# Layer 0's attention: scores computed a second time with keys on partitions, the exponential read from PSUM, and no transposes of the probabilities

## The chip, the core and the metric

The kernel runs on one NeuronCore of a Trainium2 chip. Its time is the device time of one execution in microseconds (us); the time of a kernel is the median of its runs. TensorE is called PE below, VectorE DVE, ScalarE ACT, GpSimd POOL and SyncE SP.

## The reference, cut to what matters

Two layers, each with an attention over a context and a mixture of eight experts, work on 128 sequences of 64 tokens of 128 features. The change is in the first attention, which has 16 heads of 8 features:

```python
qh = _split_heads(q @ w_q + b_q, N_HEAD)      # q = _layernorm(x)
kh = _split_heads(k @ w_k + b_k, N_HEAD)      # k = v = ctx_1024
vh = _split_heads(v @ w_v + b_v, N_HEAD)
scores = jnp.einsum('bhqd,bhkd->bhqk', qh, kh) / jnp.sqrt(jnp.float32(d_k))
attn = jax.nn.softmax(scores, axis=-1)
context = jnp.einsum('bhqk,bhkd->bhqd', attn, vh)
...
x = x + jnp.tanh(g_xattn[0]) * (context @ w_out + b_out)
```

After it come the experts of layer 0 (each token is routed to its best two), the attention of layer 1 and its experts. All is float32.

## The kernel before, in words

The 8192 tokens are 64 tiles of 128 tokens (two sequences each). The attention of layer 0 goes over `NP` = 32 pairs of tiles, in a loop `for p in range(NP + 3)` that stands once in the program of each engine, in an order written out by hand; each engine runs its own list from top to bottom, and semaphores join them. Every second turn prepares a group of four tiles: `turn` transposes the normalised tokens, `project_q` and `project_k` multiply, ACT adds the bias, and POOL's `keys` writes four masked copies of the keys into `kx`.

For a pair of tiles the work before the change is this. `scores(p)` (L474) puts queries on partitions: 16 matmuls of 32 rows and 64 columns of weights into PSUM banks 0 to 3, which hold 128 x 2048 scores. DVE takes the largest of each row of 64 keys (`largest`, L954) and subtracts it (`shift`, L961) while it copies the scores to SBUF, so that the four banks are free again for `scores(p + 1)`. ACT takes the exponential in place (`exponentials`, L1449). POOL adds the two halves of each row (`fold`, L1723), DVE sums what is left and inverts it (`denominators`, L967 and L970). PE transposes the probabilities, 16 times 128 x 128 (`turn_p`, L486), ACT copies them out of PSUM in four pieces (`copy_p`, L1456), and one turn later PE multiplies them with the values (`attend`, L501: 32 matmuls with 32 columns of weights and 64 moving columns). The reciprocals are spread by ACT (`spread_rden`, L1461), transposed (`turn_rden`, L509), copied (`copy_rden`, L1467), multiplied in (`normalise`, L976), and `output` (L516 for the bias, L520) and `add_output` (L981) end the pair. `values` is L459, `turn` L433, `turn_router0` L535 (tokens transposed for the router), `logits` L568, `project_q` L441, `project_k` L448.

Beside it DVE runs `stats0` and `stats_router` (L945, L950), and in turns 13 to 18 and 25 to 30 the steps of `route0`, which chooses the experts of the tokens that are ready; `ROUTE` says how many steps a turn gets, and where in it. From turn 19 on DVE's `put_rows` (L939) and POOL's `put` (L1734, two indirect DMAs for a tile) send out the first 16 tiles. POOL also turns sums into mean and deviation (`moments`, L1692 to L1701). Turns are named below by the `p` of `scores(p)`.

## Time and profile before

| | us |
|---|---|
| median of 3 runs | 1210.59 (1209.36 to 1211.75) |
| the profiled execution, its own time | 1206.6 |
| its span | 1204.8 |
| PE, DVE, ACT, POOL busy | 1047.8, 658.3, 641.6, 537.8 |
| first to last start of `largest` (L954) | 21.6 to 331.6 |

The span is what the instructions cover; the own time is 1.8 us more. Busy times are sums over the whole span and say little of one stage. The rows further down are read by stage: the attention of layer 0 fills the span from about 20 to 350 us.

### The profile page before, as it was taken

The page shows a single profiled execution, that of the slowest core. Times are in us where ns is not written, and L with a number is a line of the kernel's source. Part 1 is how long each engine was busy: PE and PEld are TensorE (multiplying, and loading weights), DVE is VectorE, ACT ScalarE, POOL GpSimd, SP SyncE. Part 2 cuts the span into 40 slices and gives each one's busy share as a digit, 9 for nine tenths or more (in the row PEclk, how much of TensorE's full clock was granted, in tenths as well). Part 3 has the DMA queues.
Part 4 walks back from the last instruction along what each step waited for, and adds up shares of the span by engine and source line. Part 5 has one row for each costly group of instructions (what it writes and reads, how often), then busy time and mean ns, then how long its engine had stood idle before and what let it go on. Part 6 is the DMA issues. An engine that isn't in the chain of part 4 may idle for free.

```text
span 1204.8 us, 26712 instructions
## 1 busy us (share of the span) xinstructions
PE 1047.8 (87%) x9578; PEld 882.3 (73%) x9578; DVE 658.3 (55%) x1673; ACT 641.6 (53%) x1488; POOL 537.8 (45%) x767
## 2 busy tenths in 40 slices
PE   4888877887689899999999756779999999999988
PEld 1676755665579899998998645657777877877866
DVE  3888899779955722224554746774435434533311
ACT  2888876776555454454465633435445445444433
POOL 5555664887357777723771767330220131111100
PEclk9999998998889999999999977889999999999999
DMA  9800000000045576666665211000000000000000
GB/s 375 350 2 2 3 2 2 24 22 21 10 155 176 190 231 204 188 199 194 186 202 196 110 27 35 5 1 1 1 10 15 13 10 10 10 19 9 10 18 27
DMA packets 74819, 98.30 MB, mean 82 GB/s; under 512 B 10051, under 2 KB 49219, under 8 KB 73283
## 3 DMA queue, kind: packets, MB, share of 16 engines
q1 hardware_dynamic: 65202, 75.42, 18.3%
q0 software_dynamic: 8192, 16.79, 4.7%
q10 hardware_dynamic: 1296, 4.39, 0.9%
q8 instruction: 79, 1.29, 0.4%
q14 instruction: 50, 0.40, 0.1%
HBM read 36.45 MB, written 32.11 MB: 57 GB/s over the span
## 4 chain that ended last, share of the span: by engine, by line
PE 59%; DVE 12%; ACT 9%; POOL 9%; issue 7%; DMA 2%; SPq 1%; POOLq 0%; DVEq 0%; ACTq 0%
PE psum L821 10%; PE psum L811 10%; PE psum L654 9%; PE psum L644 9%; PE psum L843 4%; POOL work L1749 3%; PE psum L792 2%; PE psum L831 2%; ACT w_sb L1449 2%; PE psum L800 2%; POOL rstd L1700 1%; DVE mx L954 1%; ACT work L1456 1%; PE psum L568 1%; PE psum L634 1%
## 5 line engine op out<-in xcount | busy, mean ns | idle before, releaser
L1539 ACT ACTIVATE hid_sb<-psum,work 128x128 f32<-128x128 f32 (+1 forms) x424 | 145.7, 411 | 146.0 <-PE psum L644 141.4
L1749 POOL DMA_INDIRECT work<-yg,place x128 | 129.4, 1011 | 105.8 <-DMA yg<-yg_sb 62.2
L1800 POOL TENSOR_TENSOR ctx_sb<-ctx_sb,chosen_sb 128x272 f32<-128x272 f32 x64 | 43.5, 681 | 292.4 <-DVE ctx_sb L1339 281.4
L644 PE MATMUL psum<-work 128*128 128x128 f32 (+1 forms) x848 | 152.0, 323 | 4.7 <-issue 2.8
L654 PE MATMUL psum<-w_sb,hid_sb 128*128 x1192 | 151.3, 276 | 0.4 <-DVE yg_sb L1146 0.4
L1641 ACT ACTIVATE work<-psum,w_sb 128x272 f32<-128x272 f32 x256 | 115.1, 487 | 65.2 <-PE psum L811 64.9
L654 PEld LDWEIGHTS psum<-w_sb,hid_sb 128*128 128x128 f32 x1192 | 145.7, 193 | 2.7 <-issue 0.6
L644 PEld LDWEIGHTS psum<-work 128*128 128x128 f32 x848 | 125.2, 194 | 14.9 <-issue 4.5
L811 PE MATMUL psum<-work,w_sb 128*128 128x272 f32 x512 | 130.1, 396 | 4.2 <-ACT work L1641 3.8
L1146 DVE TENSOR_TENSOR yg_sb<-psum,b_sb 128x128 f32<-128x128 f32 (+1 forms) x106 | 36.6, 346 | 171.7 <-PE psum L654 170.5
L821 PE MATMUL psum<-work,w_sb 128*128 128x272 f32 x512 | 127.8, 392 | 0.0
L1357 DVE TENSOR_SCALAR work<-psum,b2T_sb 128x272 f32<-128x272 f32 x64 | 32.1, 501 | 157.3 <-PE psum L821 157.3
L1723 POOL TENSOR_TENSOR fold_sb<-w_sb 128x1024 f32<-128x1024 f32 x32 | 75.5, 2361 | 83.1 <-ACT w_sb L1449 74.8
L821 PEld LDWEIGHTS psum<-work,w_sb 128*128 128x128 f32 x512 | 97.2, 190 | 20.0
L1734 POOL DMA_INDIRECT xg<-work,place x96 | 93.7, 976 | 29.7 <-issue 21.0
L811 PEld LDWEIGHTS psum<-work,w_sb 128*128 128x128 f32 x512 | 87.6, 190 | 25.7 <-ACT work L1641 5.6
L1456 ACT COPY work<-psum 128x512 f32<-128x512 f32 x128 | 69.2, 588 | 46.0 <-PE psum L486 45.1
L954 DVE TENSOR_REDUCE mx<-psum 128x32 f32<-128x2048 f32 x32 | 73.0, 2282 | 5.9 <-PE psum L474 5.7
L961 DVE TENSOR_TENSOR w_sb<-psum,mx 128x2048 f32<-128x2048 f32 x32 | 73.0, 2281 | 0.2
L1649 ACT COPY ctx_sb<-psum 102x256 f32<-102x256 f32 x64 | 23.8, 373 | 91.8 <-PE psum L831 91.6
L486 PE MATMUL psum<-ident,w_sb 128*128 128x128 f32 x512 | 71.4, 286 | 0.3 <-ACT w_sb L1449 0.3
L1422 ACT COPY lnT<-psum 128x512 f32<-128x512 f32 x64 | 37.9, 593 | 51.7 <-PE psum L433 27.9
(219 smaller groups left out, 2006.4 us busy)
## 6 DMA issues: line engine op xcount, KB each, us to landing
work<-w_sb SPq DMA_DIRECT2D x106, 258.0 KB
work<-xg SPq DMA_DIRECT2D x73, 128.0 KB
yg<-yg_sb SPq DMA_DIRECT2D x73, 128.0 KB
xg<-yg_sb SPq DMA_DIRECT2D x24, 384.0 KB, 10.5
out_x<-x_sb SPq DMA_DIRECT2D x16, 256.0 KB, 2.0
x_sb<-in_x SPq DMA_DIRECT2D x3, 1024.0 KB, 16.1
ctx_sb<-in_ctxT ACTq DMA_DIRECT2D x3, 1024.0 KB, 17.1
w_sb<-in_w1a SPq DMA_DIRECT2D x1, 2064.0 KB, 15.1
```

Of the source, the lines that this page charges most:

```text
L644: e.matmul(banks[UP_BANKS[c]][:, 0:cols], w1g_sb[:, b % NW, c * P:c * P + P], xgT_sb[:, u % 2, at:at + cols], start=True, stop=True).then_ ...
L654: ins = e.matmul(banks[DOWN_BANKS[b % 2]][:, n * D:n * D + D], hid0[:, b % 2, c, n * P:n * P + P], w2_sb[:, bass.ds(number, 1), c, :].rear ...
L811: e.matmul(banks[b][:, 0:TS * SLOTS], w1_sb[:, ex, c * P:c * P + P], xgT[sg % 2][:, ex, :, :].rearrange("p t s -> p (t s)"), start=True, s ...
L821: ins = e.matmul(banks[3][:, 0:TS * SLOTS], w2_sb[:, ex, c, :], hid[:, ex % 2, c, :, :].rearrange("p t s -> p (t s)"), start=(c == 0), sto ...
L954: e.tensor_reduce(mx[:, p % 2, :], four_banks, AX_X, ALU.max).then_inc(s_mx, 1)
L961: e.tensor_tensor(pr[:, i, :, :, :, :].rearrange("p j u h k -> p (j u h) k"), four_banks, mx[:, i, :].unsqueeze(2).to_broadcast([P, 2 * HE ...
L1456: e.copy(pT[:, p % 2, u, 4 * half:4 * half + 4, :], banks[B_T[half]]).then_inc(s_pT, 1)
L1539: e.activation(hid0[:, b % 2, c, 0:cols], banks[UP_BANKS[c]][:, 0:cols], ACT.Gelu, bias=w1g_sb[:, b % NW, HID + c:HID + c + 1]).then_inc(s ...
L1641: e.activation(hid[:, ex % 2, c, :, :].rearrange("p t s -> p (t s)"), banks[(HC * ex + c) % 3][:, 0:TS * SLOTS], ACT.Gelu, bias=w1_sb[:, e ...
L1723: e.tensor_tensor(folded, flat[:, :, 0:S // 2], flat[:, :, S // 2:S], ALU.add).then_inc(s_fold, 1)
L1734: e.indirect_dma_start(xg_dram[h], at, src, None, bounds_check=NROWS[h] - 1, oob_is_err=False).then_inc(s_put[i], 16)
L1749: e.indirect_dma_start(dst[:, k, :], None, yg_dram[h], at, bounds_check=NROWS[h] - 1, oob_is_err=False).then_inc(s_get[i], 16)
```

## The change

The scores are still computed once with queries on partitions, for their maxima only. `largest` now writes the negative maxima; PE transposes them (`turn_maxima`, one 128 x 128), DVE copies them (`copy_maxima`), and `turned_scores` computes the scores again with keys on partitions: for each of four column ranges of the four banks a matmul of a constant 0/1 table `own_max` (32 rows, 128 columns of weights, 128 moving columns, in four row groups) puts the negative maximum of each query there, and two matmuls in each row group (32 rows, 128 columns of weights from `kx`, 64 moving columns from `qT`) add the scores on top. ACT takes the exponential straight from PSUM, all four banks in one instruction, and writes the probabilities as `attend` wants them. `shift`, `turn_p`, `copy_p` and `fold` are gone. The sums over keys are now made by PE (`denominators`, 32 matmuls with the table `own_head`), DVE inverts 128 x 64 of them (`invert`), POOL spreads them over a table (`part_rden`), and a matmul with `own_dims` (`spread_rden`) takes the place of `turn_rden`. `scores(p)` now waits for the exponential of the turn before, since that is what frees banks 0 to 3. The output bias is added to the rows of x by POOL (`bias_rows`), and its matmul is gone. `add_output` comes one turn later, `attend` one turn sooner. The tables are three loads more on ACT's queue; w2 is loaded at the start instead of at the end of the attention.

```diff
             def scores(p):
                 g, i = p // 2, (p // 2) % 2
                 w.wait_ge(s_qe, g + 1)
                 w.wait_ge(s_kx, g + 1)
-                w.wait_ge(s_sub, p)
+                w.wait_ge(s_exp, p)
...
-            def turn_p(p, chunks):
-                i = p % 2
-                w.wait_ge(s_exp, p + 1)
-                for n in chunks:
-                    u, half = n // 2, n % 2
-                    w.wait_ge(s_pT, 4 * p + n - 1)
-                    for r in range(4):
-                        pair = 4 * half + r
-                        ins = e.transpose(banks[B_T[half]][:, r * P:r * P + P], pr[:, i, pair // 2, u, 2 * (r % 2):2 * (r % 2) + 2, :],
-                                          ident[:])
-                    ins.then_inc(s_pt, 1)
+            def turn_maxima(p):
+                w.wait_ge(s_mx, p + 1)
+                w.wait_ge(ld["ident"], 64)
+                e.transpose(banks[B_M][:, 0:P], mx[:], ident[:]).then_inc(s_mt, 1)
+
+
+            def turned_scores(p):
+                i = (p // 2) % 2
+                w.wait_ge(s_mT, p + 1)
+                for u in range(2):
+                    t = 2 * (p % 2) + u
+                    for h in range(2):
+                        at = 256 * u + 128 * h
+                        for quad in range(QUADS):
+                            q = slice(32 * quad, 32 * quad + 32)
+                            e.matmul(banks[quad][:, at:at + P], own_max[q, u, h, :], mxT[q, :], start=True, stop=False)
+                        for b in range(2):
+                            c = t * P + b * S
+                            for quad in range(QUADS):
+                                q = slice(32 * quad, 32 * quad + 32)
+                                ins = e.matmul(banks[quad][:, at + b * S:at + b * S + S],
+                                               kx[q, i, 2 * t + b, 2 * h:2 * h + 2, :].rearrange("p j k -> p (j k)"),
+                                               qT[q, i, c:c + S], start=False, stop=(b == 1))
+                ins.then_inc(s_sub, 1)
...
-            def turn_rden(p):
+            def denominators(p):
                 i = p % 2
-                bank = banks[B_C]
+                w.wait_ge(s_rden, p)
+                for r in range(PAIRS):
+                    for u in range(2):
+                        for b in range(2):
+                            row = 32 * (2 * u + b)
+                            ins = e.matmul(banks[B_M][row:row + 32, P:P + S], own_head[:, r, :], pT[:, i, r // 2, u, r % 2, b * S:b * S + S],
+                                           start=(r == 0), stop=(r == PAIRS - 1))
+                ins.then_inc(s_dd, 1)
+
+            def spread_rden(p):
                 w.wait_ge(s_rdm, p + 1)
-                for u in range(2):
-                    ins = e.transpose(bank[:, 256 + u * P:256 + u * P + P], rdm[:, i, u * P:u * P + P], ident[:])
-                ins.then_inc(s_av, 1)
+                e.matmul(banks[B_C[p % 2]][:, 256:512], own_dims[:, 0:P], rdm[:, p % 2, :], start=True, stop=True).then_inc(s_rt, 1)
...
             def exponentials(p):
-                flat = pr[:, p % 2, :, :, :, :].rearrange("p j u h k -> p (j u h k)")
+                flat = pT[:, p % 2, :, :, :, :].rearrange("p j u h q -> p j (u h q)")
                 w.wait_ge(s_sub, p + 1)
-                e.activation(flat, flat, ACT.Exp, scale=SCALE0).then_inc(s_exp, 1)
+                w.wait_ge(s_dd, p - 1)
+                e.activation(flat, psum[:, 0:4, :], ACT.Exp, scale=SCALE0).then_inc(s_exp, 1)
```

The order of an engine's list, as the compiled programs have it. First PE, turn 8 of the loop before, from `scores` (L474) to the transposes of the next group (L433); each row is the line, the operation, what it writes and reads, and partitions by columns of the output:

```order
L474 MATMUL psum<-work 64x256 x16
L568 MATMUL psum<-wrc,lnT 128x8 x4
L501 MATMUL psum<-work,hid_sb 32x64 x32
L459 MATMUL psum<-w_sb,ctx_sb 64x2x32 x8
L509 MATMUL psum<-ident,rdm 128x128 x2
L486 MATMUL psum<-ident,w_sb 128x128 x8
L448 MATMUL psum<-ctx_sb,w_sb 128x512
L516 MATMUL psum<-bias_sb,ones_row 128x256
L520 MATMUL psum<-w_sb,ctxn 128x128 x2
L486 MATMUL psum<-ident,w_sb 128x128 x8
L433 MATMUL psum<-ident,ln_sb 128x128 x4
```

And PE of the changed kernel, the first part of an odd turn (`scores` is L471 there, `logits` L583, `attend` L511, `turn` L430, `denominators` L523, `values` L456, `turn_maxima` L478, `turned_scores` L490 and L495):

```order
L471 MATMUL psum<-work 64x256 x16
L583 MATMUL psum<-wrc,lnT 128x8 x4
L511 MATMUL psum<-work,hid_sb 32x64 x32
L430 MATMUL psum<-ident,ln_sb 128x128 x4
L523 MATMUL psum<-work,own_head 32x64 x32
L456 MATMUL psum<-w_sb,ctx_sb 64x2x32 x8
L478 MATMUL psum<-ident,mx 128x128
L490 MATMUL psum<-mxT,own_max 128x128 x4
L495 MATMUL psum<-work 128x64 x8
```

The last two rows stand there four times in turn. Between `scores` and the maxima's transpose there is now all of `logits`, `attend`, `turn`, `denominators` and `values`; an even turn has `turn_router0` in place of `turn` and no `logits`. Behind the last of the turned scores the list goes on to the next turn (project, `spread_rden` L529, `output` L534):

```order
L495 MATMUL psum<-work 128x64 x8
L445 MATMUL psum<-ctx_sb,w_sb 128x512
L529 MATMUL psum<-rdm,own_dims 128x256
L534 MATMUL psum<-w_sb,ctxn 128x128 x2
L471 MATMUL psum<-work 64x256 x16
```

Only these three stand between the turned scores and the next `scores`, which waits for the exponential. DVE, one turn before the change:

```order
L954 TENSOR_REDUCE mx<-psum 128x32
L976 TENSOR_TENSOR ctxn<-psum,ctxn 128x256
L961 TENSOR_TENSOR w_sb<-psum,mx 128x2048
L981 SCALAR_TENSOR_TENSOR x_sb<-psum,tg_sb,x_sb 128x256
L967 TENSOR_REDUCE den<-fold_sb 128x32
L970 RECIPROCAL rden<-den 128x4x2x4
L945 BN_STATS stats<-x_sb 128x6 x2
L950 BN_STATS stats<-x_sb 128x6 x2
```

and the same turn of DVE in the changed kernel:

```order
L996 SCALAR_TENSOR_TENSOR x_sb<-psum,tg_sb,x_sb 128x256
L975 TENSOR_REDUCE mx<-psum 128x4x8
L980 COPY mxT<-psum 128x128
L985 RECIPROCAL rden<-psum 128x64
L990 TENSOR_TENSOR ctxn<-psum,ctxn 128x256
L963 BN_STATS stats<-x_sb 128x6 x2
L968 BN_STATS stats<-x_sb 128x6 x2
```

Two long passes (L961 and L967) are gone from it, a short copy and a longer reciprocal are new, and the steps of `route0` all stand behind the last row.

## Rows read from the trace of the kernel before

**Rows 1.** Windows by stage: busy us (instructions) of each engine, then granted clock, DMA.

```profile
21.62:81.60 59.98, 48.58 (x848) 36.26 (x852) 48.94 (x62) 45.75 (x85) 33.58 (x48) 0.91 0.60 235
81.60:134.64 53.04, 46.86 (x892) 37.07 (x884) 44.99 (x62) 43.37 (x82) 36.03 (x59) 1.00 0.01 2
134.64:331.65 197.01, 152.34 (x2632) 118.72 (x2624) 174.76 (x290) 130.60 (x241) 120.99 (x153) 0.92 0.04 13
331.65:354.15 22.50, 17.65 (x308) 15.15 (x298) 15.30 (x37) 12.24 (x24) 9.88 (x20) 0.95 0.52 178
```

**Rows 2.** One line's instructions: ns min/median/max, first and last start us.

```profile
L954 DVE TENSOR_REDUCE mx<-psum x32: 2261/2280/2293, 21.6 to 331.6; 128x32 f32<-128x2048 f32 x32
```

**Rows 3.** Groups by line, 50 to 330 us: busy us, mean ns, idle before.

```profile
L1723 POOL TENSOR_TENSOR fold_sb<-w_sb 128x1024 f32<-128x1024 f32 x28 | 66.1, 2360 | 62.1 <-ACT w_sb L1449 54.9 <-DVE den L967 5.1 <-issue 1.7
L961 DVE TENSOR_TENSOR w_sb<-psum,mx 128x2048 f32<-128x2048 f32 x28 | 63.9, 2281 | 0.1
L486 PE MATMUL psum<-ident,w_sb 128*128 128x128 f32 x448 | 62.2, 285 | 0.0
L1456 ACT COPY work<-psum 128x512 f32<-128x512 f32 x112 | 60.5, 588 | 43.1 <-PE psum L486 42.3
L1449 ACT ACTIVATE w_sb<-w_sb 128x2048 f32<-128x2048 f32 x27 | 51.6, 1912 | 0.0
L1715 POOL TENSOR_SCALAR work<-work,vec_sb 128x512 f32<-128x512 f32 x52 | 35.3, 694 | 16.5 <-ACT work L1434 16.3
L1734 POOL DMA_INDIRECT xg<-ln,place x32 | 32.4, 1012 | 10.2 <-issue 7.2 <-POOL nmr L1701 2.5 <-DVE ln L939 0.3
L1700 POOL TENSOR_TENSOR rstd<-ln_tmp,minus_half 128x8 f32<-128x8 f32 x12 | 20.0, 1667 | 1.0
L976 DVE TENSOR_TENSOR ctxn<-psum,ctxn 128x256 f32<-128x256 f32 x28 | 11.8, 423 | 17.6 <-ACT ctxn L1467 17.4
L970 DVE RECIPROCAL rden<-den 128x32 f32<-128x32 f32 x27 | 9.5, 353 | 0.9
```

**Rows 4.** Timeline, PE: start us, length us, instructions (records) merged, idle before.

```profile
103.09 1.12 PE L441 MATMUL psum<-lnT,w_sb 128*128 128x512 f32 x2 [0.23 <-ACT hid_sb L1443]
104.48 0.61 PE L520 MATMUL psum<-w_sb,ctxn 128*128 128x128 f32 x4
104.93 1.04 PE L486 MATMUL psum<-ident,w_sb 128*128 128x128 f32 x8
105.80 0.60 PE L535 MATMUL psum<-ident,x_sb 128*128 128x128 f32 x4
106.33 1.12 PE L474 MATMUL psum<-work 32*64 32x256 f32 x32
107.38 0.97 PEld L568 LDWEIGHTS psum<-wrc,lnT 128*128 128x128 f32 x8 [0.39 <-ACT lnT L1422]
108.37 1.10 PE L501 MATMUL psum<-work,hid_sb 128*32 128x64 f32 x64
110.12 0.69 PE L459 MATMUL psum<-w_sb,ctx_sb 128*64 128x64 f32 x16 [0.66 <-ACT lg_sb L1476]
110.74 0.44 PE L509 MATMUL psum<-ident,rdm 128*128 128x128 f32 x2
...
115.52 1.12 PE L474 MATMUL psum<-work 32*64 32x256 f32 x32
116.57 1.10 PE L501 MATMUL psum<-work,hid_sb 128*32 128x64 f32 x64
117.60 0.55 PEld L459 LDWEIGHTS psum<-w_sb,ctx_sb 128*64 128x64 f32 x16
```

**Rows 5.** Timeline, the first turns.

```profile
29.21 2.01 PE L474 MATMUL psum<-work 32*64 32x256 f32 x32
...
31.33 2.29 DVE L954 TENSOR_REDUCE mx<-psum 128x32 f32<-128x2048 f32 x1 [4.74 <-PE psum L474]
```

More of the change, by code:

```diff
@@ L588, in tensor_program @@
             for p in range(NP + 3):
[L589 removed]
                 if p < NP:
                     scores(p)
+                if p % 2 == 1 and 0 <= (p - 7) // 2:
+                    w.wait_ge(s_wrc, 1)
+                    logits((p - 7) // 2, ROUTER, B_P, wrc[:, 0:NE], s_lnTr, s_lgm, s_lg)
+                for h in range(NPARTS - 1):
+                    if p == routing_start(h) + 4:
+                        count0(h)
+                if 0 <= p - 1 < NP:
+                    attend(p - 1)
```

310 lines of the change are left out of this document (148 added, 162 removed).

## The prediction

> **What bounds the kernel now.** I read the windows by stage first. The attention of layer 0 runs from the first `largest` at 21.6 us to the last at 331.6 us: 310.0 us for 31 turns, 10.0 us each [rows 2]. It has two halves. In turns 6 to 12, where no routing runs, 53.04 us for six turns is 8.84 us a turn, and PE, DVE and ACT are all busy for 43 to 47 of the 53 us: no single engine is the bound, they hand over to each other [rows 1]. From 134.64 to 331.65 us there are 18 turns of 10.94 us, and DVE is busy for 174.76 of 197.01 us: the steps of `route0` and `put_rows` lie on top of a DVE that was already nearly full, and PE's granted clock falls to 0.92 because it waits [rows 1]. Then 22.5 us pass until the experts begin [rows 1]; everything later is untouched but for the order of a few small instructions.
>
> **What leaves the engines.** Per turn DVE loses `shift` (2.28 us) and the sum over 1024 columns (half the width, so about 1.2), ACT loses four copies of 0.588, POOL the fold of 2.36, and PE 16 transposes [rows 3]. New on DVE are a 128 x 128 copy (below the 0.42 of the 128 x 256 row L976; I take 0.3) and a reciprocal of 64 columns instead of 32 (between 0.35 and 0.71; I take 0.55) [rows 3]. DVE's quiet turn of 44.99 / 6 = 7.50 us busy becomes 7.50 - 2.28 - 1.2 - 0.35 + 0.3 + 0.55 = 4.5, ACT's 43.37 / 6 = 7.23 becomes 7.23 - 2.35 = 4.9 [rows 1]. Neither is a bound any more.
>
> **What comes onto PE.** For the pace I use the starts of neighbours in the timeline [rows 4]. `scores` takes 1.05 us of PE's list (115.52 to 116.57), `attend` 1.03 (116.57 to 117.60), `logits` 0.99 (107.38 to 108.37), four transposes 0.53 when another tile shape follows (105.80 to 106.33), `values` 0.62 (110.12 to 110.74). `denominators` has the form of `attend` (32 columns of weights, 64 moving columns, 32 of them): 1.03. A matmul of 512 moving columns is 0.86 (its record of 1.12 less the tail of about 0.25 that others show), so `spread_rden` with 256 is 0.43, and `output` 0.45 (104.48 to 104.93).
>
> `turned_scores` has no like in the trace. A float32 matmul leaves two records, and small shapes run side by side in as many places as the array can be cut into: L474 has 32 records of 256 moving columns in eight places, so four rounds, and lasts 1.12; L501 has 64 records of 64 columns in four places, 16 rounds, and lasts 1.10. That is 0.216 us for a round of 256 columns and 0.056 for one of 64, plus a tail near 0.2 [rows 4]. The turned scores are 48 matmuls, 96 records in four places: 8 rounds of 128 moving columns (0.11 each) and 16 of 64. If the moving columns set the pace, they last 8 x 0.11 + 16 x 0.056 + 0.2 = **1.95 us**. But each of them loads 128 columns of weights, where L474 loads 64 and L501 only 32. The nearest row for many weights and few moving columns is L568: 8 loads of 128 columns in front of only 8 moving columns take 0.97 us, 0.11 a record, although eight moving columns are nearly nothing [rows 4]. With that pace all 24 rounds cost 0.11: 2.66 + 0.2 = **2.85 us**. I take this one, since L568 is the only row in which the loads are the longer part. The upper end is that the loads of the four row groups don't run side by side either: 96 x 0.11 = 10.5 us. L474 speaks against it: 32 loads in a row of half that width (0.055) would be 1.8 us, and the whole of it lasted 1.12.
>
> The skill has a rule that would make this worse. The Trainium skill ("TensorE: Matmul & The Clock Gate", Part 3, What overlaps and what doesn't) says that a weight load overlaps a running matmul only where the row group differs; each row group here reloads for its own next matmul. By that rule a round costs load plus matmul, 0.11 + 0.11 or 0.11 + 0.056. The trace does not agree: in L520 the four records of 128 columns, all in the same rows, follow each other in 0.45 us, 0.11 each, with loads as wide as the matmuls [rows 4].
>
> **The new loop.** Before, banks 0 to 3 were free after `shift`; now one turn holds them until the exponential has read them. So one turn is a closed chain, and nothing of the next turn's scores can start sooner: `scores`, what stands behind them on PE, the maxima's transpose, the copy, the turned scores, the exponential. `largest` itself ends 1.1 + 2.3 = 3.4 us after the start of `scores`, sooner than PE gets to the transpose:
> - even turn: 1.05 + 1.03 + 0.53 + 1.03 + 0.62 = 4.26 us (3.73 in turns 2 and 4, which turn nothing for the router); odd turn from 7 on, with `logits`: 5.25.
> - then transpose 0.28, copy 0.3, turned scores 2.85, exponential 1.91 [rows 3, 4] and four or five handovers, 0.14 in all: 5.48.
> - the project, the spread and the output (0.86 + 0.43 + 0.45 = 1.74) lie under the exponential; without that cover they would cost those 1.74.
>
> Sum: **9.74 us** for an even turn, **10.73** for an odd one from 7, 9.21 in turns 2 and 4, against 8.84 in the quiet stretch and 10.94 in the routed one.
>
> Turn 0 is longer. Its turned scores run while PE has the 1.2 GHz level, at which L474 took 2.01 instead of 1.12 [rows 5]: about 5.3 us. Behind them stand, one after another, the group's transpose copy, `project_k`, its bias, `project_q` and `scores(1)`, which the old list had done under DVE's work: 2.3 + 0.55 + 0.3 + 5.3 + 1.95 + 0.6 + 1.5 + 0.7 + 1.5 + 1.3 = 16 us instead of the 9.7 between the first two `largest` (21.62 and 31.33) [rows 1, 5].
>
> The steps of `route0` stand behind DVE's statistics, where DVE has 3.7 us (odd to even) to 4.6 us free in a turn. In the routed half a turn has 174.76 / 18 = 9.71 us of DVE against 7.50, 40 us in all for 24 steps and 16 rows put out [rows 1]; that is 1.5 us a step, two steps a turn, so the mean turn fits and only the heaviest don't. I count 4 us that stick out (between 0 and 10). POOL in the same turns does keys (4 x 0.694), the bias rows and `part_rden` (a half and a quarter of the width of the 2.36 row: 1.2 and 0.6), moments in every second turn (the power alone is 1.67, with nine small operations about 4), and 2.5 indirect DMAs of 1.3 (1.01 and 0.32 of idle time before each) [rows 3]: 8 us a turn on average. `part_rden` is wanted by PE only at 8.4 us into the turn, and in the worst of four turns (moments, puts and keys one after another) I get it done at 8.2: hidden, but by 0.2 us.
>
> Turns: 16 + 2 x 9.21 + 4 x 9.74 (turns 1, 3, 5, 6) + 12 x 9.74 + 12 x 10.73 + 4 = **323 us against 310.0: 13 us more**.
>
> **The rest at nothing.** The end (22.5 us until the experts) loses the bias matmul and the w2 load that stood in SP's queue ahead of the tokens; it gains the way over POOL to the last reciprocals, behind 4 us of moments. I count zero, within 3 us either way. The three tables (0.45 MB) come on ACT's queue while all is loading anyway, ahead of context that is wanted later. On the profile's own time that is 1206.6 + 13 = 1220; the median of the runs shown stands 4.0 above that execution, so 1210.6 + 13 = **1223.6 us**.
>
> **The rivals.**
> 1. *The weight loads hide.* Turned scores at 1.95: each turn is 0.9 shorter, 27 us in all; 5 of them come back, since DVE then has 0.9 us less for the routing steps and POOL is late by the same. 1223.6 - 27 + 5 = **1202**, faster. It decides at about 2.3 us for the turned scores. For it: in every small shape of the trace the moving columns set the pace. Against it: none of these has loads wider than its moving columns but L568. Chance 0.20.
> 2. *Nothing overlaps in a row group* (the rule above), or loads run partly in a row: 8 x 0.22 + 16 x 0.166 + 0.2 = 4.6 us, 1.75 more in each of 31 turns, **1278** and up. Chance 0.06.
> 3. *POOL is late.* `spread_rden` stands on PE in front of the next `scores`; if moments and puts are slower than I reckon, all engines wait for `part_rden` in one or two of four routed turns, 1 to 2 us each: 10 us, **1234**. Chance 0.10.
> 4. *The routed half gains more.* PE has no long waits now and keeps the 2.4 GHz level, and my chain may count a tail twice; 0.4 us less a turn brings it to **1211**, no change. Chance 0.06.
> The forecast itself: 0.58, with 1215 to 1233 as its own range.
>
> **Numbers.** Less than 0.2% (2.4 us) can't be told from no change here. Faster: rival 1 and a part of 4, 0.22; same 0.06; slower 0.72. Range: 1199, which takes in rival 1, to 1238, which takes in rival 3.
>
> **What would show it.** Right: records of L495 start 0.11 us apart per round and `turned_scores` lasts 2.8 to 2.9; quiet turns are 9.7 and 10.7 in turn; PE waits for DVE's `mxT` and for ACT's exponential, once each a turn; DVE under 60% in the quiet stretch; routed turns hardly longer than quiet ones. Wrong: rounds of L495 at 0.056 (rival 1), PE waiting for `rdm` (rival 3), or `turn_maxima` waiting long for `largest`, which would mean that PE's first part is shorter than I count.

## The result and the profile after

The changed kernel takes **1256.1 us** (median of 4 runs, 1254.6 to 1259.1) against 1210.9 us for the kernel before on the same chip: a ratio of **1.038, 95% interval 1.036 to 1.040**. The prediction was 1223.6 us with a range to 1238. Slower was right; the loss is 45 us and not 13. In the first two sets of experiments below (e1 to e4, then a1, e5, c1 and n1) the experts' part of each profiled kernel took about 175 us longer (the kernel before: 1391.2 and 1389.9 us as a whole), so there I read ratios within a set and quiet turns only.

From the page of the changed kernel: its busy times and the queue q8, which carries instructions (packets, MB, share):

```profile
span 1252.8 us, 35706 instructions
PE 1120.9 (89%) x14154; PEld 949.1 (76%) x14154; DVE 557.2 (44%) x1642; ACT 569.3 (45%) x1328; POOL 503.8 (40%) x783
q8 instruction: 115, 1.88, 0.6%
```

DVE has 101 us less to do and ACT 72 us less, as the change wants. PE has 73 us more: 14154 matmul records in place of 9578. The same page of the kernel before has 79 packets and 1.29 MB on q8, where this one has 115 and 1.88.

The windows by stage of the changed kernel (columns as in [rows 1]): the first three turns, turns 3 to 12, turns 13 to 30, and from the last `largest` to the experts:

```profile
22.75:71.00 48.25, 37.81 (x725) 27.73 (x729) 11.29 (x20) 17.23 (x29) 19.07 (x39) 0.72 0.84 337
71.00:173.10 102.10, 97.15 (x2865) 79.29 (x2853) 45.85 (x91) 48.95 (x81) 39.71 (x75) 1.00 0.01 4
173.10:372.05 198.95, 183.49 (x5204) 149.72 (x5203) 110.64 (x260) 86.47 (x146) 94.66 (x154) 0.98 0.04 12
372.05:399.40 27.35, 19.63 (x426) 17.83 (x426) 13.36 (x42) 5.45 (x11) 11.56 (x21) 0.78 0.24 84
```

In turns 3 to 12 PE is busy for 97 of 102 us, with DVE and ACT under half; in [rows 1] three engines shared the time. Set beside the prediction's own sum, stage by stage (us of the profiled executions; a turn runs from one start of `largest` to the next):

| stage | before | forecast | after |
|---|---|---|---|
| to the first `largest` | 21.6 | 21.6 | 22.7 |
| turns 0 to 2 | 25.5 | 35.0 | 48.2 |
| turns 3 to 12 | 87.6 | 99.8 | 102.1 |
| turns 13 to 30 | 197.0 | 188.2 | 199.0 |
| last `largest` to the experts | 21.1 | 21.1 | 27.4 |
| experts and layer 1 | 852.0 | 852.0 | 853.4 |

"To the experts" ends here with PE's first transposes for them, at 352.75 us before and 399.35 after; the 22.5 us of the prediction and of [rows 1] run to the second ones, at 354.15. Of the 48 us between the two profiled executions 22.7 lie in the first three turns, 14.5 in turns 3 to 12, 2.0 in turns 13 to 30, 6.3 behind them and 2.5 in the start and the experts.

PE's timeline of one even turn of the changed kernel, to be held against [rows 4]:

```profile
98.88 1.12 PE L471 MATMUL psum<-work 32*64 32x256 f32 x32 [0.16 <-ACT work L1458]
99.93 1.10 PE L511 MATMUL psum<-work,hid_sb 128*32 128x64 f32 x64
100.96 0.66 PE L550 MATMUL psum<-ident,x_sb 128*128 128x128 f32 x4
101.55 1.10 PE L523 MATMUL psum<-work,own_head 128*32 128x64 f32 x64
102.58 0.74 PE L456 MATMUL psum<-w_sb,ctx_sb 128*64 128x64 f32 x16
103.26 0.33 PE L478 MATMUL psum<-ident,mx 128*128 128x128 f32 x1
103.97 0.50 PE L490 MATMUL psum<-mxT,own_max 32*128 32x128 f32 x8 [0.39 <-DVE mxT L980]
104.29 0.57 PE L495 MATMUL psum<-work 32*128 32x64 f32 x16
104.69 0.46 PE L490 MATMUL psum<-mxT,own_max 32*128 32x128 f32 x8
...
106.81 1.12 PE L438 MATMUL psum<-lnT,w_sb 128*128 128x512 f32 x2
107.77 0.59 PE L529 MATMUL psum<-rdm,own_dims 128*128 128x256 f32 x2
108.20 0.61 PE L534 MATMUL psum<-w_sb,ctxn 128*128 128x128 f32 x4
108.87 1.12 PE L471 MATMUL psum<-work 32*64 32x256 f32 x32
```

And DVE and ACT in the same turn:

```profile
103.62 0.29 DVE L980 COPY mxT<-psum 128x128 f32<-128x128 f32 x1 [1.23 <-PE psum L478]
```

```profile
106.94 1.88 ACT L1458 ACTIVATE work<-psum 128x2048 f32<-128x2048 f32 x1 [1.93 <-PE psum L495]
```

The turned scores last 2.84 us (103.97 to 106.81); six rounds of four row groups, one block of L490 and L495, take 0.67 to 0.72, and the last block 0.78 to the start of L438. The transpose starts at 103.26, the copy at 103.62, the exponential ends at 108.82 and the next `scores` starts at 108.87: the closed chain, link by link. PE has little idle time in it. From the transpose to L490 it is 0.71 us where the transpose takes 0.28, and L534 is done at about 108.65 if it takes the 0.45 us of L520 in [rows 4]: 0.43 and 0.22 us of 9.99 are idle. So PE's own list of this turn is about 9.3 us, by itself longer than a whole quiet turn before (8.84).

Two stages came out far from the forecast: the first three turns and the end. First PE in turns 1 and 2, the first two rows from turn 1:

```profile
45.41 0.49 PE L490 MATMUL psum<-mxT,own_max 32*128 32x128 f32 x4 [0.38 <-DVE mxT L980]
47.18 0.38 PE L490 MATMUL psum<-mxT,own_max 32*128 32x128 f32 x2 [1.28 <-issue]
...
58.72 0.30 PE L523 MATMUL psum<-work,own_head 128*32 128x64 f32 x3 [2.28 <-issue]
...
60.94 0.97 PE L495 MATMUL psum<-work 32*128 32x64 f32 x16
```

PE stops in the middle of a row of equal matmuls, and nothing that the profile shows releases it. I read these as times in which PE's own instructions come late and call them stops of its supply; no row shows that wait itself. Behind the second one the records of L495 take 0.97 in place of 0.57. The same stretch in windows of 10 us, with the granted clock and the share of the DMA engines third and second from the end:

```profile
40.00:50.00 10.00, 8.33 (x261) 6.92 (x245) 3.88 (x6) 2.20 (x5) 1.13 (x2) 0.87 1.03 409
50.00:60.00 10.00, 6.54 (x184) 4.38 (x183) 2.47 (x2) 3.03 (x4) 3.94 (x5) 0.98 1.04 408
60.00:70.00 10.00, 9.65 (x120) 7.94 (x128) 1.91 (x6) 4.24 (x7) 4.07 (x11) 0.50 0.25 92
```

The DMA engines are full to 60 us, and after it PE has the 1.2 GHz level.

PE's waits of the changed kernel from 72 to 405 us (total, times, longest):

```profile
PE psum L490 <- DVE mxT L980: 11.1, 29, 0.4
PE psum L529 <- POOL rdm L1726: 7.8, 3, 3.9
PE psum L471 <- ACT work L1458: 4.0, 15, 1.0
```

The longest of the second kind, on PE and on POOL:

```profile
387.83 1.22 PE L529 MATMUL psum<-rdm,own_dims 128*128 128x256 f32 x2 [3.92 <-POOL rdm L1726]
388.85 1.06 PE L534 MATMUL psum<-w_sb,ctxn 128*128 128x128 f32 x4
```

```profile
379.40 1.71 POOL L1695 TENSOR_TENSOR rstd<-ln_tmp,minus_half 128x8 f32<-128x8 f32 x1
...
382.19 1.11 POOL L1738 DMA_INDIRECT xg<-ln,place  x1 [0.79 <-POOL nmr L1696]
...
386.16 0.97 POOL L1738 DMA_INDIRECT xg<-ln,place  x1 [0.30 <-issue]
387.15 0.63 POOL L1726 TENSOR_TENSOR rdm<-rden,own_dims 128x256 f32<-128x256 f32 x1
```

The reciprocals are ready at 384.87 (L985 of DVE: 0.56 us from 384.31); POOL comes to them only behind the moments and four puts, and PE runs at half clock afterwards (L534: 1.06 in place of 0.61).

### The profile page after: what moved, and what is told of

It is laid out like the page before. It is cut to its first block, busy times and chain, and to the rows that moved or that the text cites. A ratio compares the mean times of both kernels' runs of the same rounds, so it can differ in the third digit from the quotient of the medians.

```text
span 1252.8 us, 35706 instructions
## 1 busy us (share of the span) xinstructions
PE 1120.9 (89%) x14154; PEld 949.1 (76%) x14154; DVE 557.2 (44%) x1642; ACT 569.3 (45%) x1328; POOL 503.8 (40%) x783
## 3 DMA queue, kind: packets, MB, share of 16 engines
q8 instruction: 115, 1.88, 0.6%
## 4 chain that ended last, share of the span: by engine, by line
PE 72%; POOL 7%; ACT 6%; DVE 6%; issue 5%; DMA 3%; SPq 1%; ACTq 0%; POOLq 0%; DVEq 0%
PE psum L660 10%; PE psum L670 10%; PE psum L839 9%; PE psum L829 9%; PE psum L861 4%; ACT work L1458 4%; PE psum L495 4%; PE psum L490 3%; PE psum L471 3%; PE psum L511 3%; PE psum L523 2%; PE psum L583 2%; POOL work L1753 2%; PE psum L810 2%; PE psum L849 2%
## 5 line engine op out<-in xcount | busy, mean ns | idle before, releaser
L829 PEld LDWEIGHTS psum<-work,w_sb 128*128 128x128 f32 x512 | 87.6, 190 | 26.0 <-ACT work L1636 6.5
L1458 ACT ACTIVATE work<-psum 128x2048 f32<-128x2048 f32 x32 | 60.1, 1877 | 68.9 <-PE psum L495 68.9
L1726 POOL TENSOR_TENSOR rdm<-rden,own_dims 128x256 f32<-128x256 f32 x32 | 19.6, 613 | 144.1 <-DVE rden L985 109.3
L495 PE MATMUL psum<-work 32*128 32x64 f32 x2048 | 77.0, 265 | 0.0
L490 PE MATMUL psum<-mxT,own_max 32*128 32x128 f32 x1024 | 63.3, 313 | 13.6 <-DVE mxT L980 12.3
L495 PEld LDWEIGHTS psum<-work 32*128 32x128 f32 x2048 | 73.5, 196 | 0.0
## 6 DMA issues: line engine op xcount, KB each, us to landing
x_sb<-in_x SPq DMA_DIRECT2D x3, 1024.0 KB, 11.8
```

Source lines behind the costliest of these rows:

```text
L490: e.matmul(banks[quad][:, at:at + P], own_max[q, u, h, :], mxT[q, :], start=True, stop=False)
L495: ins = e.matmul(banks[quad][:, at + b * S:at + b * S + S], kx[q, i, 2 * t + b, 2 * h:2 * h + 2, :].rearrange("p j k -> p (j k)"), qT[q, i ...
L829: e.matmul(banks[b][:, 0:TS * SLOTS], w1_sb[:, ex, c * P:c * P + P], xgT[sg % 2][:, ex, :, :].rearrange("p t s -> p (t s)"), start=True, s ...
L1458: e.activation(flat, psum[:, 0:4, :], ACT.Exp, scale=SCALE0).then_inc(s_exp, 1)
```

## The experiments

The expectations below set a theory 1 against a theory 2. Theory 1 is the prediction's closed chain with three terms mis-sized: PE starved at the start while the DMA engines are full, POOL late at the end, and small handovers. Its rivals were that moving columns or an overlap of loads set the price of the turned scores, that PE's longer list alone starves it, and that some engine other than PE would be the bound once the chain is gone.

### The price of the turned scores

**e3_double_moving.** The weights stay; each matmul of L495 moves 128 columns in place of 64, so that the other sequence's queries are added into the same sums.

```diff
-                            c = t * P + b * S
+                            c = t * P
...
-                                ins = e.matmul(banks[quad][:, at + b * S:at + b * S + S],
+                                ins = e.matmul(banks[quad][:, at:at + P],
...
-                                               qT[q, i, c:c + S], start=False, stop=(b == 1))
+                                               qT[q, i, c:c + P], start=False, stop=(b == 1))
```

> The changed kernel, but each of the 32 turned-score matmuls streams 128 columns of queries instead of 64, over the same 128 columns of weights, so that the scores are sums over both sequences (the computation is changed there). Theory 1 (the load of 128 columns of weights sets the pace of the second scores, 0.11 us a round): the moving columns double at no cost, turned scores stay at 2.9 us, 1256 within 3 us. Theory 2 (the moving columns set it, and 2.9 us has another reason): 16 rounds grow by 0.056, 0.9 us a turn, 28 us in all, 1284.

Measured: ratio 1.047 (1.043 to 1.051), beside 1.042 for e1 and e4 of the same set. PE's timeline:

```profile
100.94 0.50 PE L490 MATMUL psum<-mxT,own_max 32*128 32x128 f32 x8 [0.39 <-DVE mxT L980]
101.27 0.62 PE L495 MATMUL psum<-work 32*128 32x128 f32 x16
...
103.83 1.12 PE L438 MATMUL psum<-lnT,w_sb 128*128 128x512 f32 x2
```

From L490 to L438 it is 2.89 us with twice the moving columns of L495, against 2.84. The moving columns are free here. That the 128 columns of weights set the pace follows only by comparison with the 0.056 us a round of L501 [rows 4], which has 32 columns of weights; no run narrows the weights in this shape.

**e6_no_own_max.** The 16 matmuls of L490 are left out, so the maxima are found and turned but not subtracted.

```diff
-                        for quad in range(QUADS):
-                            q = slice(32 * quad, 32 * quad + 32)
-                            e.matmul(banks[quad][:, at:at + P], own_max[q, u, h, :], mxT[q, :], start=True, stop=False)
...
-                                               qT[q, i, c:c + S], start=False, stop=(b == 1))
+                                               qT[q, i, c:c + S], start=True, stop=True)
```

> The changed kernel without the own_max matmuls alone: 16 fewer a turn, the maxima are still taken, turned and copied, and PE still waits for the copy, but they aren't subtracted. Theory 1 (a matmul of the turned scores costs its weight load, 0.11 us a round of four, whatever it moves): 8 of 24 rounds go, 0.9 us a turn; quiet turns 9.05 and 10.1, the whole 25 to 29 us faster than the changed kernel, a ratio to the kernel before of 1.014 to 1.020. Theory 2 (the load of a constant table overlaps with what is running, since it waits for nothing): less than 0.5 us a turn.

Measured: 1233.8 us, ratio 1.0205 (1.018 to 1.023). In its timeline the turned scores go from 106.96 to 108.91:

```profile
106.96 2.01 PE L492 MATMUL psum<-work 32*128 32x64 f32 x64 [0.38 <-DVE mxT L977]
108.91 1.12 PE L445 MATMUL psum<-ctx_sb,w_sb 128*128 128x512 f32 x2
```

1.95 us for 16 rounds, so 8 rounds cost 0.89: the rounds that load the constant table cost as much as the others. Quiet turns are 9.05 and 10.1 as expected. The whole gains 21 us and not 25 to 29 (1.038 to 1.0205): POOL is still late at the end, with turns of 17.7 and 17.0 us between exponentials there, where the changed kernel has 12.5 and 16.9 (its three waits for `rdm` are 9.7 us, for 7.8).

**e4_values_between.** `values` behind `turn_maxima` on PE.

```diff
                 if p < NP:
+                    turn_maxima(p)
                     values(p)
-                    turn_maxima(p)
                     turned_scores(p)
```

> The changed kernel with one edit: the eight matmuls of the values (0.61 us) stand on PE between the transpose of the maxima and the turned scores instead of ahead of the transpose. Nothing is left out. Theory 1 (each turn is a closed chain, and PE idles about 0.7 us for the transpose's result and DVE's copy): the values move into that gap; about 0.55 us less in each of 30 turns, 1256 becomes about 1240. Theory 2 (PE is full and the gap is only its drain): no change, 1254 to 1258.

Measured: ratio 1.042 (1.039 to 1.045); quiet turns of 9.5 and 10.55 us in place of 9.95 and 11.0. PE's wait for `mxT` is gone. The gap was on the path: 0.45 us a turn. What that brings the whole (16 us were expected) can't be read here: no run of the changed kernel as it is stands in this set, and in the next one it has 1.048.

### The first three turns

**e2_fills_late.** w2 (2 MB) and the 27 zero fills (9.5 MB) wait until four turns are through.

```diff
             load("b2", b2_sb[:], t_in["b2"])
+            w.wait_ge(s_sub, 4)
             load("w2", w2_sb[:], t_in["w2a"])
```

> The changed kernel with one edit: the load of w2 (2 MB) and the zero fills of the token buffers (9 MB) wait on SP's queue until the turned scores of turn 3 are done, so that the DMA engines are nearly idle from about 35 us on. Nothing is left out. Theory 1 (PE's instructions come late while the DMA engines are full: the two waits of 1.28 and 2.28 us for nothing that the profile names, and the fall of PE's clock to the 1.2 GHz level behind the second): turns 1 and 2 fall from 13.9 and 16.3 us to about 11 and 9.5, the time from 1256 to about 1247. Theory 2 (turns 0 to 2 are long because of their own serial order and of a clock that falls whatever the DMA does): no change, 1254 to 1258.

Measured: ratio 1.050 (1.046 to 1.054). The first three turns are 40.1 us instead of 48 (turns 1 and 2: 11.9 and 10.2), but turns 4 to 6 are 15.6, 11.7 and 11.8, so the gain that I expected of the whole did not come. Its waits of PE from 72 to 110 us, and the window of that load:

```profile
PE psum L491 <- issue: 3.1, 1, 3.1
PE psum L496 <- issue: 1.5, 1, 1.5
```

```profile
80.00:100.00 20.00, 15.76 (x335) 12.47 (x336) 4.58 (x9) 6.65 (x9) 0.61 (x1) 0.83 1.03 409
```

The idle times went with the load: moved, not removed.

**b1_two_more_mb.** In the kernel before, 2 MB more are loaded at the start.

```diff
             load("b2", b2_sb[:], t_in["b2"])
+            w.wait_ge(ld["w1"], 16)
+            load("w1", w1_sb[:], t_in["w1a"])
```

> The kernel before, with nothing of the change in it but one thing: 2 MB more are loaded at the start (the first layer's w1 a second time, into the same place, behind the first), as the changed kernel has 2 MB of w2 and 0.45 MB of tables more there. Theory 1 (the first turns of the changed kernel are long because its loads fill the DMA engines longer, and PE's own instructions come over the same engines): the first three turns, 25.5 us before, become 30 us or more, with idle time of PE that nothing releases. Theory 2 (the old list has half of the PE records per turn, so it survives the same load; it takes both, the load and the longer list): the first three turns stay within 2 us of 25.5, the whole within 2 us of the kernel before.

Measured: 1210.2 against 1209.8 us, ratio 1.0005 (0.999 to 1.002). Its DMA engines are as full to 60 us as those of the changed kernel:

```profile
50.00:60.00 10.00, 8.55 (x146) 6.22 (x145) 9.41 (x12) 8.42 (x17) 6.96 (x12) 1.00 1.04 409
```

and its first three turns are 25.5 us as before, without one idle time of PE's supply. PE ran 146 matmul records in that window; the changed kernel ran 184 in spite of its stop, and the thin version below ran 277. Theory 1 as I put it here (the load alone) is refuted; it takes the load and the new list. The other traces agree. All twelve with the full load and a list of the new kind (n1 and n2 below among them) have a longest stop of 1.4 to 3.1 us; the kernel before, b1 and b2 have none over 0.5.

**e8_thin_loads.** The changed kernel with w2 in eight pieces and the fills one by one, two pieces a turn.

```diff
-            load("w2", w2_sb[:], t_in["w2a"])
+            for k in range(NE):
+                w.wait_ge(s_sub, 2 + k // 2)
+                load("w2", w2_sb[:, k], t_in["w2a"][:, k])
...
+                    w.wait_ge(s_sub, 6 + filled // 2)
+                    filled += 1
                     e.dma_start(rows[:, at:at + n], zeros[:, 0:n]).then_inc(s_fill, 16)
```

> The changed kernel with the same loads, spread thin: w2 in eight pieces and the 27 zero fills of SP one after another, two pieces a turn from turn 2 to 19, in place of all at once behind the first loads. Theory 1 (PE's instructions came late in turns 1 and 2 only because the DMA engines were full there; a full minute of loads starves the longer list, a thin one doesn't): the idle times of 1.28 and 2.28 us that nothing releases are gone and appear nowhere later, the clock is back by 45 us, the first three turns are 38 to 42 us in place of 48.2, and the rest stays: a ratio to the kernel before of 1.028 to 1.033. Theory 2 (starvation comes from the length of PE's list alone): the idle times stay or move, less than 4 us are gained.

Measured: 1252.0 against 1211.3 us, ratio 1.034 (1.032 to 1.036), just above the 1.028 to 1.033 expected. The first three turns are 38.9 us, in place of 48.2. Its window, and all that is left of idle supply in it:

```profile
50.00:60.00 10.00, 8.26 (x277) 6.79 (x278) 3.89 (x7) 3.15 (x7) 6.71 (x15) 1.00 0.11 37
```

```profile
PE psum L528 <- issue: 0.7, 1, 0.7
```

So 9.3 us of the 13 that the first turns had too much come from the loads: 3.6 us of stopped supply (1.28 and 2.28), of which 0.7 stays, and 6.4 us of what followed them. The largest piece of it that rows show is the slower clock: the turned scores of turn 2 took 5.3 us (60.35 to 65.68) for 2.84. The size changes with the kernel: with `part_rden` on DVE and the full load the first three turns are 44.0 to 46.2 us (e7, e5, e1), and thinning takes 4.7 us (c1 44.0, c2 39.3). The other stages stay; the experts' part of this profiled execution was 2 us longer, and the ratio moved by less than the stage did.

### The end of the attention

**e1_spread_on_dve, e5_spread_on_dve_again, e7_spread_on_dve_3.** One kernel, three times: `part_rden` is taken from POOL's list and stands behind `invert` on DVE.

```diff
                 if 0 <= p - 1 < NP:
                     invert(p - 1)
+                    part_rden(p - 1)
```

> The changed kernel with one edit: the multiplication that spreads the reciprocals (128 x 256, 0.61 us on POOL) stands on DVE, right behind the reciprocal, instead of on POOL behind its moments and indirect DMAs. Nothing is left out. Theory 1 (POOL is late): three turns of the changed kernel wait 7.8 us on PE for POOL's part, and PE is at half clock for some 8 us behind them; these go, 1256 becomes about 1240, and the end of the attention (last maxima to first expert) falls from 28.7 to about 22 us. Theory 2 (the 32 us beyond the forecast lie elsewhere, in the first turns and in the per-turn chain): at most 3 us are gained, 1253 or more. The first three turns stay at 48 us in either.

> The changed kernel, but the spreading of the reciprocals (part_rden) is done by DVE right behind the inversion, not by POOL; nothing else moves. Theory 1 (POOL was late at the end of the attention: some 8 us of PE waits for rdm, and about 8 us more of half clock that these waits brought with them): the waits of L529 are gone, the tail between the last largest and the experts goes from 27.4 to 20 to 23 us, turns 13 to 30 together are 0 to 4 us shorter, the whole is 8 to 16 us faster than the changed kernel. Theory 2 (the tail is longer because the attention's last turn is longer itself, and POOL's late turns only stand beside it): the tail stays at 26 or more and the whole is within 4 us.

> The changed kernel with part_rden on DVE instead of POOL, for a reading of the end of the attention where the experts take the 852 us that they take in the profile of before. Theory 1 (POOL was late there): no wait of L529, the 12.5 and 16.9 us turns at the end become ordinary ones of 10 to 11, the stretch from turn 13 to the experts goes from 226.4 to 212 to 218 us, a ratio to the kernel before of 1.024 to 1.031. Theory 2 (the moments themselves, or the routing steps, hold these turns): the waits change their name only (L490 for mxT behind routing steps), less than 4 us are gained, a ratio of 1.034 or more.

Measured: ratios 1.0415 (1.037 to 1.046), 1.046 (1.042 to 1.049) and 1.030 (1.027 to 1.033). **a1_after_again** is the changed kernel as it is, once more, to measure the second set by:

> The changed kernel as it is, once more, as the ruler for the three that run beside it. Both theories: the ratio to the kernel before is 1.036 to 1.042, quiet turns of 9.95 and 11.0 us, first three turns 46 to 49 us, the routed stretch near 199 us, 27 to 29 us between the last largest and the experts.

It gave 1.048 (1.045 to 1.051), outside what was expected, with quiet turns of 10.0 to 10.5 and 11.0. The second try can't be told from it; in a1 PE had 28 short stops of its supply between 150 and 390 us, 9.4 us in all, where the first profile of the changed kernel has one of 0.4. The third, beside a kernel before of 1211.3 us, decides: turns 13 to 30 take 195.1 us (199.0), the tail 23.0 (27.4), 8.3 us together, and of PE's 7.8 us of waits for `rdm` 1.1 are left (I had expected none):

```profile
PE psum L529 <- DVE rdm L992: 1.1, 1, 1.1
```

POOL was late. Two more stages of this profiled execution differ, and not by the wait: the first three turns are 4.2 us shorter (44.0) and the experts' part 5.7 us longer (859.1), which nothing here explains.

### The three together

**c1_spread_and_values** is e1 and e4 in one; **c2_spread_values_thin** adds e8.

> The changed kernel with two edits: part_rden on DVE as in the run beside it, and values behind turn_maxima on PE in place of ahead of it, so that PE has 0.6 us of work while DVE copies the maxima. Theory 1 (each turn is a closed chain and PE's idle time for mxT is part of it): quiet turns are 9.5 and 10.55 us, 0.45 us shorter than 9.95 and 11.0, and over 30 turns 12 to 14 us come on top of what the spread alone gives: 20 to 30 us faster than the changed kernel, a ratio to the kernel before of 1.012 to 1.022. Theory 2 (in the routed turns DVE or POOL sets the pace, so the gap there is free): only the ten or so quiet turns gain, 5 us on top of the spread alone.

> The changed kernel with three edits: part_rden on DVE, values behind turn_maxima, thin loads. If theory 1 holds for each (POOL late at the end, an exposed gap for mxT, a starved start), they add up: 9 + 13 + 8 us, 30 in all, a ratio of 1.008 to 1.016 to the kernel before, still slower than it, since the closed chain of 9.5 and 10.5 us stays. The rival that the change was slow by these three alone would give 1.00 or less.

Measured: c1 1.039 (1.033 to 1.044), beside 1.046 for the spread alone: quiet turns 9.49 and 10.55, as said; the whole missed the 1.012 to 1.022 that I expected; how much of that is the condition of the set is open. c2: 1230.1 us, ratio **1.016 (1.014 to 1.018)**, at the upper end of what was expected. Its stages: 39.3, 99.1, 186.9, then 22.4 to the experts. With all three mended the attention from the first to the last `largest` is 325 us (before 310). Against the kernel before, the first three turns have 13.8 us too much and turns 3 to 12 have 11.5; turns 13 to 30 are 10.1 us shorter. So what keeps c2 slower is the start, turn 0 above all (18.7 us for 9.7), and the quiet turns, where PE's list and the chain over it are nearly the same length; over all turns from 3 on the new loop costs 1.4 us. One stop of supply of over 1 us is left, 1.1 us until 74.2 us, just behind a piece of the load: the DMA share is 0.75 from 71 to 72 us and 0.00 from 73 to 74.

### Without the maxima

**n1_no_maxima, n2_values_first, n3_values_first_thin.** These leave out `scores`, `largest`, the transpose, the copy and `own_max`, and take the exponential of unshifted scores; `turned_scores` opens the turn. n2 puts the lists in another order, n3 adds the thin loads. A turn runs here from one exponential to the next, as there is no `largest`.

```diff
                 if p < NP:
-                    scores(p)
+                    turned_scores(p)
+                    values(p)
...
-                    turn_maxima(p)
-                    turned_scores(p)
```

> The changed kernel without the maxima: the first scores (L471), largest (L975), the transpose of the maxima, its copy and the own_max matmuls are all left out, and the exponential is taken of the scores without a shift (which cancels in the softmax). The turned scores stand first in PE's turn and wait only for the exponential of the turn before; part_rden is on DVE. Theory 1 (the change is slow because one closed chain of PE work, transpose, copy, turned scores and exponential fills the turn, not because PE or any engine is full): the chain left is turned scores (16 rounds of 0.11 us and a tail, 1.95 us) and exponential (1.93), about 4.1 us, which all other PE work covers or follows; a turn is PE's own list, 6.9 us even and 7.9 odd, in place of 9.95 and 11.0, the first three turns 35 to 40 us, the attention some 90 to 105 us shorter, the whole 1150 to 1170 us where the changed kernel takes 1256, faster than the kernel before by 3 to 5%. Theory 2 (PE's supply of instructions or DVE's routing work is the real bound of the second half): quiet turns shrink as said, but routed turns stay above 9.5 us, and the whole is 1190 or more.

> The version of the changed kernel without maxima (n1_no_maxima), with PE's and ACT's lists put in another order: values directly behind the turned scores and copied ahead of the exponential, attend ahead of logits, and the project at the end of the turn, so that no matmul waits for the copy of a bank just written (0.84 us a turn there). Theory 1 (PE's own list sets the turn once no chain does): quiet turns are 7.0 to 7.4 and 8.0 to 8.4 us, where n1_no_maxima had 8.22 and 9.23, the attention 20 to 30 us shorter than there, a ratio to the kernel before of 0.97 to 1.0. Theory 2 (in the second half it is not PE's list but the supply of its instructions, or the routing chain between PE, ACT, DVE and POOL): quiet turns shorten as said, routed ones stay at 10.9, and less than 12 us are gained.

> n2_values_first (no maxima, list reordered) with the loads spread thin as well. Theory 1: the first three turns go from 35.1 to 29 to 32 us, nothing else moves, the ratio to the kernel before is 0.970 to 0.974. Theory 2 (without the maxima PE's list is short enough to live with full DMA engines): no gain, 0.977.

Measured: n1 1.015 (1.011 to 1.019), n2 **0.977 (0.9745 to 0.979)**, n3 **0.973 (0.970 to 0.976)**, 1178.0 us. n1's quiet turns were 8.2 and 9.2 where I expected 6.9 and 7.9: PE waited 0.84 us a turn for the copy of `values`, and I had left that handover out. Its whole missed by more: 3 to 5% faster was expected and 1.5% slower measured, with routed turns of 11.0 us, as its theory 2 has it. PE of n2:

```profile
101.47 2.02 PE L473 MATMUL psum<-work 32*128 32x64 f32 x64
103.42 0.69 PE L456 MATMUL psum<-w_sb,ctx_sb 128*64 128x64 f32 x16
...
105.96 0.66 PE L528 MATMUL psum<-ident,x_sb 128*128 128x128 f32 x4
107.16 0.70 PE L507 MATMUL psum<-rdm,own_dims 128*128 128x256 f32 x2 [0.55 <-DVE rdm L956]
...
108.14 1.02 PE L438 MATMUL psum<-lnT,w_sb 128*128 128x512 f32 x2
109.10 2.01 PE L473 MATMUL psum<-work 32*128 32x64 f32 x64
```

A turn of 7.63 us is PE's own list and one wait (expected: 7.0 to 7.4). Turns 13 to 30 take 152.4 us, 8.5 each, in spite of all the routing. That shows that PE's list sets the turn once no chain does. It does not show that the chain was what made the changed kernel slow, as n1's theory 1 had it: of the 2.36 us between 9.99 and 7.63, 2.2 are matmuls that are no longer there (`scores` 1.05, the transpose 0.28, eight rounds 0.89). How much of the way from n1 to n2 is the order and how much the condition of the second set stays open: quiet turns, which that condition leaves alone, explain only about 10 us. Thin loads brought n3 2.3 us in the first turns (35.1 to 32.8, where I expected 29 to 32), and its one stop of 1.4 us is gone; the two intervals overlap.

**b2_before_no_maxima.** The kernel before without `largest` and `shift`; the exponential reads PSUM and comes early in ACT's turn; transposes, copies and fold stay.

```diff
-                w.wait_ge(s_sub, p + 1)
-                e.activation(flat, flat, ACT.Exp, scale=SCALE0).then_inc(s_exp, 1)
+                w.wait_ge(s_sc, p + 1)
+                w.wait_ge(s_pt, 4 * (p - 1))
+                w.wait_ge(s_fold, p - 1)
+                e.activation(flat, psum[:, 0:4, :], ACT.Exp, scale=SCALE0).then_inc(s_exp, 1)
```

> The kernel before without the maxima: largest and shift are left out, ACT takes the exponential of the unshifted scores straight from PSUM (which cancels in the softmax), ahead of the copies of its turn; the transposes of the probabilities, their copies and the fold stay. Theory 1 (what filled a turn before was DVE's two passes over the scores and the handovers around them, not the transposes): DVE loses 4.56 us a turn, PE's own list of about 7.3 us sets the turn, quiet turns are 7.3 to 7.9 in place of 8.84, routed ones 8 to 9 in place of 10.94, the attention 45 to 75 us shorter, a ratio to the kernel before of 0.94 to 0.965; the version without the transposes beside it gains nothing over this one. Theory 2 (the transposes and their copies are the cost, as the change has it): the turns stay above 8.5 everywhere and less than 20 us are gained.

Measured: 1199.8 us, ratio 0.991 (0.989 to 0.993): 10 us of the 45 to 75 that I expected, and about a third of the 28.6 us that n2 has over the kernel before (1209.8 to 1181.2). Theory 1 missed, and theory 2 holds but for its quiet turns (7.8 us in place of 8.5 and more). Routed turns did not change: 194.4 and 194.3 us for the 18, both from exponential to exponential (197.0 in the table above is from `largest` to `largest`). Its window of 60 us there, below that of the kernel before:

```profile
180.00:240.00 60.00, 47.18 (x848) 37.47 (x846) 51.22 (x89) 39.63 (x74) 37.60 (x48) 0.91 0.04 13
```

```profile
180.00:240.00 60.00, 50.66 (x877) 40.17 (x876) 29.14 (x75) 43.63 (x83) 44.30 (x59) 0.91 0.04 15
```

DVE falls from 51 to 29 us busy and the pace stays. So a full DVE was not what made the routed half long; handovers between PE, ACT, DVE and POOL and the lower clock in the waits remain as causes, which no run here takes apart. b2 also adds a link of its own: its `scores` waits for the exponential, as in the changed kernel.

## Why the prediction was right and wrong

**Right.** The turned scores: 2.85 forecast, 2.84 measured, for the reason given, rounds of 0.11 us; rival 1 (1.95) is refuted by e3 and e6. The rule that rival 2 took from the Trainium skill ("TensorE: Matmul & The Clock Gate", Part 3, What overlaps and what doesn't) would have given 4.6 us here, by the prediction's estimate; the trace of the changed kernel does not bear it out in this shape: four row groups of load and matmul advance by 0.11 us a round. The closed chain is there, link by link, and with 10.0 and 11.0 us it was right to add it up. What the prediction did not say is that PE's list of a turn (about 9.3 us) is nearly as long as the chain, so that a shorter chain alone could gain no more than about 0.7 us a turn. A sign of it: it expected PE to wait for the exponential once each turn, and from 72 to 405 us there are 15 such waits, 4.0 us in all.

**Too small, per turn: 0.26 us.** Forecast 9.74 and 10.73, measured 10.0 and 11.0. The links from the transpose to the next `scores` took 5.61 us (103.26 to 108.87) for my 5.48, the part ahead of it 4.38 for 4.26: L550 and L456 take 0.59 and 0.68 where I had 0.53 and 0.62. That is 2.3 us in turns 3 to 12 and about 5 in turns 13 to 30.

**The step that failed: turns 0 to 2.** "The three tables (0.45 MB) come on ACT's queue while all is loading anyway" costed the loads at nothing and did not speak of the 2 MB of w2 ahead of the fills. It was 13.2 us too little (48.2 for 35.0). e8 takes 9.3 us of them back by thinning the load; b1 shows that the same load does nothing to the shorter list. So the cost of the load together with the new list is shown; that it is PE's own instructions that come late stays a reading. The other 4 us are turn 0 (17.8 in e8 for 16: its projects took 2.05 and 2.08, for my 1.5; the granted clock there reads 1.00 in e8 and 0.50 in the changed kernel with the same two times, so this row can't be relied on so early), `center_router`, for which PE waited 1.15 us, and the handovers.

**The other step that failed: "hidden, but by 0.2 us".** I had spread the puts evenly, 2.5 a turn. The changed list (`rows_by`: five tiles in four turns, two puts a tile) gives four of them to one turn in four and two to the others. In the worst turn shown above the moments and four puts stand ahead of `part_rden`, and PE waits 3.9 us for it. That was rival 3 (10 us, chance 0.10), and e7 sizes it at 8.3 us in the stages, half in turns 13 to 30, half in the tail. With it falls "I count zero, within 3 us" for the tail: 6.3 us, of which 4.4 are POOL's.

**Wrong about the kernel before.** "The steps of `route0` and `put_rows` lie on top of a DVE that was already nearly full" had the busy time right, but a full DVE is not what held these turns, as b2 shows. It did not decide the number, since I took the routed turns of the new kernel from its chain.

Together: 13.2 + 2.3 + 10.8 (turns 13 to 30) + 6.3 + 2.5 (start and experts) = 35 us, the difference between 13 and 48 us of the two profiled executions.

## What to carry to other kernels

Before passes are moved from DVE and ACT onto PE, ask which engine has the time: here PE went from 9578 to 14154 records, and its own list of a quiet turn, 9.3 us, became longer than the whole turn had been. Matmuls that load 128 columns of weights to move 64 cost as much as if they moved 128. When a buffer is freed later than before, add up the closed chain, then look for work that can stand in each of its gaps; `values` in the gap of the maxima's copy was worth 0.45 us a turn. And loads that were harmless may not be so any more under a new list: cost them anew, and look at the worst turn of a shared engine, not at its average.

The maxima are computed for a shift that cancels, and `scores`, their transpose and their subtraction are 2.2 us of PE's turn. The version without them and without the transposes, with `part_rden` on DVE, its lists in another order and thin loads, is 2.7% faster than the kernel before; it is only to be had where the scores are known to stay far from the exponential's limits.

## What the runs showed of the hardware that was not expected

- With 32 rows and 128 columns of weights in four row groups, 64 or 128 moving columns take the same time: 2.84 and 2.89 us for the whole.
- At a DMA share of 1.03 to 1.04 PE of the changed kernel stood for 1.3 and 2.3 us, and in e2 for 3.1, with nothing to release it. The kernel before with the same load (b1, 1.02 to 1.04 from 40 to 60 us) never did. In the thin version c2 there was one such stop of 1.1 us, and from 73 to 74 us, within it, the share was 0.00: a stop can outlast the load.
- Behind the second stop the granted clock fell to 0.50, and the records of L495 went from 0.57 to 0.97 us: the turned scores of that turn alone lost 2.5 us by it, more than the 2.3 us of the stop.
